# One transformer block, 16 chunks: the next chunk's first layer norm moves to the end of the current slot, and the query products open each slot

## The chip, the core and the metric

The kernel runs on one core of a Trainium2 chip. Its engines are TensorE (PE: matrix products and transposes into PSUM), VectorE (DVE), ScalarE (ACT), GpSimd (POOL) and SyncE (SP: the DMA queue). Each engine takes its own list of instructions in order; they meet at semaphores. The metric is the device time of one execution in microseconds (us).

## The reference

A cross-attention block on x (8, 1024, 512) with a context of 64 rows per batch, 16 heads of 32, and a feed-forward width of 2048:

```python
q = _layer_norm(query, ln1_g, ln1_b)
qh = (q @ wq + bq).reshape(Bq, Sq, H, hd)
kh = (context @ wk + bk).reshape(Bq, Sc, H, hd)
vh = (context @ wv + bv).reshape(Bq, Sc, H, hd)
scores = jnp.einsum('bqhd,bkhd->bhqk', qh, kh) * scale
scores = jnp.where(allowed[None, None, :, :], scores, NEG_INF)
probs = jax.nn.softmax(scores, axis=-1)
o = jnp.einsum('bhqk,bkhd->bqhd', probs, vh).reshape(Bq, Sq, Dm)
x = query + (o @ wo + bo)
h = _layer_norm(x, ln2_g, ln2_b)
return x + jax.nn.gelu(h @ w1 + b1, approximate=False) @ w2 + b2
```

## The kernel before

The 8192 rows of x are cut into 16 chunks of 512 rows, and a chunk into four tiles t of 128 rows. The program is a row of 17 slots. Slot c does the attention half of chunk c and, beside it, the feed-forward half of chunk c-1; slot 0 has attention only, slot 16 feed-forward only. Two slots (an even and an odd chunk) make one batch and one turn of a hardware loop. Products are in float16 with each operand split in a high and a low part, so that a product takes three matmuls per block of 128 rows.

A slot runs over 18 groups g. In group g TensorE does F1(g), the first feed-forward product (12 matmuls at line 989, g below 16), and F2(g-2), the second one (12 matmuls at line 1193, g from 2). Between them stand the attention steps. The table `PLAN` gives each step a position: position 2g comes after F1(g), position 2g+1 after F2(g-2). Every engine walks the same table, so it sets the order on all of them. The steps are, for each tile or head group t:

- T: the normalised rows `xhat` of chunk c are transposed (line 1032, four transposes), copied by ScalarE (line 578) and split by VectorE (line 711 into `act_T`). `xhat` has two buffers.
- Q: query products; S: scores, with VectorE's row maxima and subtraction (lines 920, 922); E: ScalarE's exponentials (line 590), VectorE's sums (line 927), and GpSimd's division (line 485, `normalise`).
- Z: transposes of the probabilities; V: products with the values; O: output product, residual and the statistics of the second norm; H: transposes of the second norm's rows, like T.

After the step at position 2g, VectorE splits the gelu of group g (lines 962 and 711); F2(g) waits for that. Called "the split of g" below.

The first norm of chunk c is done by VectorE at the very start of slot c, ahead of position 0: for each tile `norm_stats` (lines 687, 689, 692), then GpSimd's power in `rstd_of` (line 421), then `norm_apply` (line 707) into `xhat`. For tiles 0 and 1 `norm_apply` follows the statistics two tiles later; for tiles 2 and 3 it follows T(0) and T(1), since the buffers must be read first. GpSimd's adding of the output bias to x (line 480) stands behind these norms, and with each new batch also the building of its key and value blocks (lines 464, 473). At the end of a slot VectorE adds the feed-forward result to the residual (line 976, four instructions).

Slot 1 also does the last conversions of the weights, at positions given by `conversions_at`.

Of the kernel before, what the change touches and what calls it, by code (L numbers as in the profile page):

```python
# [22 lines left out]
BATCH = 8  # L23
# [6 lines left out]
TT = CHUNK // P  # L30
HALF = CHUNK // 2
NCHUNK = BATCH * SQ // CHUNK
# [18 lines left out]
LAG = 2  # L51
GROUPS = NJ + LAG
PLAN = {
# [8 lines left out]
}  # L62

PLAN_FIRST = {
# [7 lines left out]
}  # L72
W2_SUMS_AT = (0, 1, 20, 21)

# [11 lines left out]
def cross_attention_block(nc, x, context, wq, wk, wv, bq, bk, bv, wo, bo,  # L86
# [5 lines left out]
    with ExitStack() as ctx:  # L92
# [72 lines left out]
        x_sb = sb("x_sb", [P, TT, D], F32)  # L165
# [94 lines left out]
        x_loaded = [sem(f"x_loaded{t}") for t in range(TT)]  # L260
# [58 lines left out]
        def plan(c, position):  # L319

            return (PLAN_FIRST if isinstance(c, int) and c == 0 else PLAN).get(position, [])

        def halves(c, t):


            return ff2_ps[:, 0:2, :] if isinstance(c, int) and c == 0 and t % 2 else at_ps[:, :, :]

        def slots(eng, slot, loads=False):


            slot(0, 0, True, False, 0)
            slot(1, 1, True, True, None)
            with eng.Fori(0, BATCH - 1 - loads) as i:
                slot(2 * i + 2, 0, True, True, i + 1)
                slot(2 * i + 3, 1, True, True, None)
            if loads:
                slot(NCHUNK - 2, 0, True, True, BATCH - 1)
                slot(NCHUNK - 1, 1, True, True, None)
            slot(NCHUNK, 0, False, True, None)

        block = ctx.enter_context(nc.Block())
# [1 line left out]
        @block.sync  # L343
        def _(sp):
            sp.dma_start(ctx_raw, ctx_rows).then_inc(ctx_loaded, 16)
            sp.dma_start(wk_raw, wk.rearrange("(k p) n -> p k n", p=P)).then_inc(w_loaded[W_K], 16)
            row = 0
            for v in (bq, bk, ln1_g, ln1_b, ln2_g, ln2_b, b1):
                n = v.shape[0] // P
                sp.dma_start(vec_rows[row:row + n, :], v.rearrange("(k p) -> k p", p=P)).then_inc(vecs_loaded, 16)  # L350
                row += n
            sp.dma_start(wv_raw, wv.rearrange("(k p) n -> p k n", p=P)).then_inc(w_loaded[W_V], 16)
            sp.dma_start(bv_row, bv.rearrange("(a n) -> a n", a=1).to_broadcast([P, D])).then_inc(bv_loaded, 16)
            sp.dma_start(wq_raw, wq.rearrange("(k p) n -> p k n", p=P)).then_inc(w_loaded[W_Q], 16)
            for t in range(TT):
                sp.dma_start(x_sb[:, t], x_tiles[t]).then_inc(x_loaded[t], 16)
            for v, dst in ((bo, bo_row[:, :]), (b2, b2_row[:, :])):
                sp.dma_start(dst, v.rearrange("(a n) -> a n", a=1).to_broadcast([P, D])).then_inc(rows_loaded, 16)
            sp.dma_start(wo_raw, wo.rearrange("(k p) n -> p k n", p=P)).then_inc(w_loaded[W_O], 16)
            for n in range(N1):  # L360
                sp.dma_start(w1_raw[n], w1[:, n * D:(n + 1) * D].rearrange("(k p) n -> p k n", p=P)
                             ).then_inc(w_loaded[W_1 + n], 16)

            def load_w2(n):
                sp.dma_start(w2_raw[n], w2[n * D:(n + 1) * D, :].rearrange("(k p) n -> p k n", p=P)
                             ).then_inc(w_loaded[W_2 + n], 16)

            for n in W2_ORDER[:2]:
                load_w2(n)

            def move_values(n, batches):


                even, odd = slice(batches.start, batches.stop, 2), slice(batches.start + 1, batches.stop, 2)
                sp.wait_ge(kv_out, KT + batches.stop // 2)
                for a in range(2):
                    for half in (slice(0, SC), slice(SC, P)):
                        sp.dma_start(v_sb[half, a, odd, :], v_sb[SC:P, a, even, :]).then_inc(v_moved, 16)
                sp.wait_ge(v_moved, (6 * n + 4) * 16)
                for a in range(2):  # L380
                    sp.dma_start(v_sb[SC:P, a, even, :], v_sb[0:SC, a, even, :]).then_inc(v_moved, 16)

            move_values(0, slice(0, 2))
            move_values(1, slice(2, BATCH))
            for n in W2_ORDER[2:]:
                load_w2(n)

            def slot(c, par, attn, ff, batch):
                if not isinstance(c, int) or c < NCHUNK - 1:
                    for t in range(TT):  # L390
                        sp.wait_ge(x1_set, 4 * c + t + 1)
                        sp.dma_start(x_sb[:, t], x_tiles[4 * c + (TT + t)]).then_inc(x_loaded[t], 16)
                if ff:
                    for t in range(TT):
                        sp.wait_ge(out_set, 4 * c + (t + 1 - TT))
                        sp.dma_start(out_tiles[4 * c + (t - TT)], x1[1 - par][:, t]).then_inc(out_stored[t], 16)

            slots(sp, slot, loads=True)
            for t in range(TT):
                sp.wait_ge(out_stored[t], 16 * NCHUNK)  # L400

        @block.gpsimd
        def _(pool):
# [48 lines left out]
            def slot(c, par, attn, ff, batch):  # L452
                if not attn:
                    return
                first = isinstance(c, int) and c == 0
                if not first:
                    for t in range(TT):
                        rstd_of(c, t)

                def key_blocks():  # L460

# [56 lines left out]
                for t in range(TT):  # L518
                    rstd_of(c, TT + t)
                    if t:  # L520
                        add_b2(t - 1)
                add_b2(TT - 1)

            slots(pool, slot)

        @block.scalar
        def _(act):
# [104 lines left out]
            def slot(c, par, attn, ff, batch):  # L632
                first = isinstance(c, int) and c == 0
                for g in range(GROUPS):
                    if first and 2 * g == BIAS_ROWS_AT:
                        bias_rows(1, D, bias_rows_sb)
                    if first and 2 * g == CONV_FROM:
                        act.wait_ge(scales_ready[2], 1)
                    if ff and g < NJ:
                        act.wait_ge(ff1_done, NJ * c + (g + 1 - NJ))  # L640
                        if g >= 2:
                            act.wait_ge(g_lo, NJ * c + (g - 1 - NJ))
                        else:
                            wait(act, g_lo, NJ * c + (-NJ))
                        nc.scalar.activation(gelu_full[g % 2], ff1_ps[:, g % 2, :], ACT.Gelu,  # L645
                                             bias=b1p[:, g:g + 1], scale=col(C1)).then_inc(g_full, 1)
                    for position in (2 * g, 2 * g + 1):
                        if attn:
                            for kind, t in plan(c, position):
                                step(c, par, kind, t)  # L650
                        for n in conversions_at(c, position):
                            convert(n)
                        if first and position in W2_SUMS_AT:
                            n = W2_SUMS_AT.index(position)
                            magnitudes(W_2 + W2_ORDER[n], n + 1)
                if first:
                    act.wait_ge(scales_ready[3], 1)
# [4 lines left out]
        def _(dve):  # L662
# [228 lines left out]
                    convert(n)  # L891

            def slot(c, par, attn, ff, batch):
                if attn and not (isinstance(c, int) and c == 0):
                    for t in range(TT):
                        dve.wait_ge(x_loaded[t], 16 * (c + 1))
                        norm_stats(c, t, x_sb[:, t])
                        if t >= 2:
                            norm_apply(c, t - 2, x_sb[:, t - 2])

                def step(kind, t):
                    bank = at_ps[:, t % 2, :]
                    tiles = bank.rearrange("p (k n) -> p k n", k=KT)
                    if kind == "T":
                        T_step(c, t)
                    elif kind == "H":
                        dve.wait_ge(h_hi, 4 * c + t + 1)
                        rows = slice(t * P, (t + 1) * P)
# [73 lines left out]
        def _(pe):  # L982
# [93 lines left out]
            def slot(c, par, attn, ff, batch):  # L1076
                def step(kind, t):
                    bank = at_ps[:, t % 2, :]
                    rows = slice(t * P, (t + 1) * P)
                    if kind == "T":  # L1080
                        T_step(c, t)
                    elif kind == "W":
                        values(t)
                    elif kind == "Q":
# [137 lines left out]
```

## Time and profile before

| | us |
|---|---|
| median of three runs (2073.62 to 2075.64) | 2074.24 |
| the profiled execution's own time | 2073.56 |
| its span in the trace | 2071.8 |
| TensorE busy | 1942.1 (94%) |
| VectorE busy | 1291.9 (62%) |
| ScalarE busy | 589.0 (28%) |
| GpSimd busy | 452.9 (22%) |

The chain that ended last is 73% TensorE and 16% VectorE. Matmuls are pipelined: a group's busy times overlap, so distances between starts are what a block costs. In the timeline the number in brackets behind a row is how long the engine sat idle before it, and what released it.

### The profile page before, as it was taken

How to read it: one execution, taken by the hardware profiler on the slowest of the kernel's cores; microseconds unless marked ns; L12 is line 12 of the kernel's file. 1: busy time of each engine (PE TensorE's matmuls, PEld its weight loads, DVE VectorE, ACT ScalarE, POOL GpSimd, SP SyncE). 2: the span in 40 equal slices, each digit the busy share in tenths (PEclk: the TensorE clock that was granted, in tenths of full speed). 3: DMA queues.
4: the chain of work that ended last, by engine and by line, in shares of the span. 5: the costliest groups of instructions: out<-in, count | busy, mean ns of one | idle time of the engine just before them, and what ended most of it. 6: DMA issues, size and time to landing. Idle time of an engine off the chain costs nothing.

```text
span 2071.8 us, 28444 instructions
## 1 busy us (share of the span) xinstructions
PE 1942.1 (94%) x11206; PEld 965.0 (47%) x11206; DVE 1291.9 (62%) x1972; ACT 589.0 (28%) x820; POOL 452.9 (22%) x380
## 2 busy tenths in 40 slices
PE   4679999999999999999999999999999999999999
PEld 2334445445444444544445454544544454454444
DVE  5777766665656675666666566676666666556542
ACT  3544323232232312223232222313213231222311
POOL 2430231311222131211412022131122214111210
PEclk7879999999999999999999999999999999999999
DMA  7110000101000010000101000010100001000000
GB/s 259 37 56 1 16 26 1 41 1 31 12 11 31 1 42 1 21 21 6 36 1 41 1 21 22 1 41 1 42 1 16 26 1 42 1 23 19 1 21 21
DMA packets 27648, 51.32 MB, mean 25 GB/s; under 512 B 2536, under 2 KB 4112, under 8 KB 27536
## 3 DMA queue, kind: packets, MB, share of 16 engines
q1 hardware_dynamic: 27536, 49.58, 7.3%
q8 instruction: 101, 1.65, 0.3%
q14 instruction: 11, 0.09, 0.0%
HBM read 31.22 MB, written 16.78 MB: 23 GB/s over the span
## 4 chain that ended last, share of the span: by engine, by line
PE 73%; DVE 16%; issue 5%; ACT 3%; DVEq 2%; POOL 0%; DMA 0%; SPq 0%; POOLq 0%; ACTq 0%
PE ff_ps L1193 25%; PE ff_ps L989 24%; PE at_ps L989 15%; PE at_ps L1032 4%; DVE ssum L927 3%; DVE arena L962 3%; PE at_ps L1136 2%; PE at_ps L1110 2%; DVE arena L711 2%; DVEq L688 2%; DVE act_T L711 1%; DVE xhat L707 1%; ACT L590 1%; DVE arena L976 1%; ACT arena L590 1%
## 5 line engine op out<-in xcount | busy, mean ns | idle before, releaser
L1193 PE MATMUL ff_ps<-w_all,arena 128*128 128x512 f16 x3072 | 706.8, 380 | 31.4 <-DVE arena L711 27.1
L989 PE MATMUL ff_ps<-arena,w_all 128*128 128x512 f16 x3072 | 706.8, 381 | 3.9 <-issue 2.3
L1193 PEld LDWEIGHTS ff_ps<-w_all,arena 128*128 128x128 f16 x3072 | 295.5, 98 | 375.2 <-DVE arena L711 30.4
L989 PEld LDWEIGHTS ff_ps<-arena,w_all 128*128 128x128 f16 x3072 | 297.4, 98 | 349.8 <-issue 15.7
L645 ACT ACTIVATE arena<-ff_ps,b1p,scales 128x512 f32<-128x512 f32 x256 | 199.1, 778 | 852.4 <-PE ff_ps L989 762.6
L711 DVE SCALAR_TENSOR_TENSOR arena<-arena,scales 128x512 f16<-128x512 f32 x256 | 279.3, 1091 | 9.1
L485 POOL TENSOR_TENSOR arena<-arena,rsum 128x1024 f32<-128x1024 f32 x64 | 122.7, 1949 | 694.7 <-DVE rsum L930 694.7
L421 POOL TENSOR_TENSOR rstd<-ve,minus_half 128x1 f32<-128x1 f32 x128 | 90.6, 708 | 708.4 <-DVE ve L692 700.7
L962 DVE TENSOR_SCALAR arena<-arena,scales 128x512 f16<-128x512 f32 x256 | 159.8, 624 | 69.6 <-ACT arena L645 69.6
L711 DVE SCALAR_TENSOR_TENSOR arena<-at_ps,arena 128x512 f16<-128x512 f32 x188 | 123.8, 686 | 109.6 <-ACT arena L596 57.3
L989 PE MATMUL at_ps<-wo_hi,act_T 128*128 128x512 f16 x512 | 162.2, 379 | 1.5 <-DVE act_T L711 1.5
L989 PE MATMUL at_ps<-act_T,wq_hi 128*128 128x512 f16 x512 | 152.4, 379 | 7.2 <-DVE act_T L711 7.2
L914 DVE CAST qT<-arena 128x512 f16<-128x512 f32 x64 | 27.3, 427 | 199.2 <-ACT arena L583 199.2
L947 DVE SCALAR_TENSOR_TENSOR arena<-at_ps,scales,x_sb 128x512 f32<-128x512 f32 x64 | 48.0, 751 | 142.2 <-PE at_ps L989 142.2
L920 DVE TENSOR_REDUCE smax<-at_ps 128x16 f32<-128x1024 f32 x62 | 75.8, 1222 | 76.1 <-PE at_ps L1110 76.1
L1032 PE MATMUL at_ps<-ident,xhat 128*128 128x128 f32 x512 | 81.0, 282 | 44.6 <-DVE xhat L707 37.9
L711 DVE SCALAR_TENSOR_TENSOR act_T<-at_ps,act_T 128x512 f16<-128x512 f32 x128 | 85.3, 685 | 55.6 <-ACT act_T L602 55.6
L927 DVE TENSOR_REDUCE ssum<-arena 128x16 f32<-128x1024 f32 x64 | 75.3, 1177 | 54.1 <-ACT arena L590 54.1
L583 ACT ACTIVATE arena<-at_ps,bqp,scales 128x512 f32<-128x512 f32 x64 | 49.8, 778 | 198.2 <-PE at_ps L989 198.2
L480 POOL TENSOR_TENSOR x_sb<-x_sb,bo_row 128x512 f32<-128x512 f32 x64 | 95.7, 1513 | 19.8 <-DVE xhat L707 19.6
L1032 PEld LDWEIGHTS at_ps<-ident,xhat 128*128 128x128 f32 x512 | 63.4, 144 | 73.6 <-DVE act_T L711 26.0
L989 PE MATMUL at_ps<-act_T,wq_lo 128*128 128x512 f16 x256 | 97.0, 379 | 0.0
(136 smaller groups left out, 1595.0 us busy)
## 6 DMA issues: line engine op xcount, KB each, us to landing
x_sb<-in_x SPq DMA_DIRECT2D x64, 256.0 KB, 2.6
out_x<-arena SPq DMA_DIRECT2D x64, 256.0 KB, 2.2
w_all<-in_L_xattn_w SPq DMA_DIRECT2D x6, 1024.0 KB, 15.2
arena<-in_L_xattn_w SPq DMA_DIRECT2D x2, 1024.0 KB, 14.0
v_sb<-v_sb SPq DMA_DIRECT2D x6, 192.0 KB, 3.0
arena<-in_ctx SPq DMA_DIRECT2D x1, 1024.0 KB, 5.4
arena<-in_L_xattn_wk SPq DMA_DIRECT2D x1, 1024.0 KB, 8.1
arena<-in_L_xattn_wv SPq DMA_DIRECT2D x1, 1024.0 KB, 7.6
```

The lines of the kernel that those rows point to most:

```text
L421: nc.gpsimd.tensor_tensor(rstd[:, n:n + 1], ve[:, n:n + 1], minus_half[:, :], ALU.pow).then_inc(ln_rstd, 1)
L480: nc.gpsimd.tensor_tensor(x_sb[:, t], x_sb[:, t], bo_row[:, :], ALU.add).then_inc(xb_set, 1)
L485: nc.gpsimd.tensor_tensor(pr, pr, rsum[:, t, :].unsqueeze(2).to_broadcast([P, HEADS, SC]), ALU.mult).then_inc(p_norm, 1)
L583: nc.scalar.activation(q_full[t % 2], bank, ACT.Identity, bias=bqp[:, t:t + 1], scale=col(CQ)).then_inc(q_out, 1)
L645: nc.scalar.activation(gelu_full[g % 2], ff1_ps[:, g % 2, :], ACT.Gelu, bias=b1p[:, g:g + 1], scale=col(C1)).then_inc(g_full, 1)
L711: nc.vector.scalar_tensor_tensor(lo, src, factor, hi, ALU.mult, ALU.subtract).then_inc(done, 1)
L920: nc.vector.tensor_reduce(smax[:, t, :], scores, AX_X, ALU.max).then_inc(s_max, 1)
L927: nc.vector.reduce_sum(ssum[:, t, :], probs[t].rearrange("p (h k) -> p h k", k=SC), AX_X).then_inc(s_sum, 1)
L962: nc.vector.tensor_scalar(pair[:, 0, :], gelu_full[g % 2], col(SG), None, ALU.mult).then_inc(g_hi, 1)
L989: last = nc.tensor.matmul(out_ap, s, m, start=(i == 0), stop=(i == n - 1))
L1032: last = nc.tensor.transpose(bank[:, k * P:(k + 1) * P], source[:, k * P:(k + 1) * P], ident[:, :])
L1193: last = nc.tensor.matmul(ff2_ps[:, t, :], pair[:, s, rows], m[:, j], start=(j == 0 and i == 0), stop=(j == NJ - 1 and i == 2))
```

## The change

Slot c no longer begins with its own first norm. A new kind of step, M, does `norm_stats` of the next chunk's tile t and, from tile 2, `norm_apply` of tile t-2. M stands at positions 30 and 31, and the T steps of the next chunk at 32 to 35. With positions 0 to 5 free of T, the query products open the slot, and all the other steps come three positions earlier. Since positions move by an odd number, a step that stood behind F1 now stands behind F2 and the other way round. GpSimd's four powers for the next chunk come behind its last work of the second norm. Slot 0 gets M and T of chunk 1 at positions 27 and 28. The last chunk has no next one, so the last attention slots are now written out on every engine, and the loop has six turns.

```diff
 PLAN = {
-    2: [("T", 0)], 4: [("T", 1)], 5: [("T", 2), ("T", 3)],
-    6: [("Q", 0)], 7: [("Q", 1)], 8: [("Q", 2)], 9: [("Q", 3)],
...
+    0: [("Q", 0)], 2: [("Q", 1)], 4: [("Q", 2)], 5: [("Q", 3)],
...
+    27: [("H", 1)], 28: [("H", 2)], 30: [("H", 3), ("M", 0), ("M", 1)],
+    31: [("M", 2), ("M", 3)],
+    32: [("T", 0)], 33: [("T", 1)], 34: [("T", 2)], 35: [("T", 3)],
 }
...
+    27: [("M", 0), ("M", 1), ("M", 2), ("M", 3)],
+    28: [("T", 0), ("T", 1), ("T", 2), ("T", 3)],
...
+        def has_next(c):
+
+            return not isinstance(c, int) or c < NCHUNK - 1
...
-            with eng.Fori(0, BATCH - 1 - loads) as i:
+            with eng.Fori(0, BATCH - 2) as i:
...
-                if not first:
-                    for t in range(TT):
-                        rstd_of(c, t)
...
                 add_b2(TT - 1)
+                if has_next(c):
+                    for t in range(TT):
+                        rstd_of(c + 1, t)
...
-                if attn and not (isinstance(c, int) and c == 0):
-                    for t in range(TT):
-                        dve.wait_ge(x_loaded[t], 16 * (c + 1))
-                        norm_stats(c, t, x_sb[:, t])
-                        if t >= 2:
-                            norm_apply(c, t - 2, x_sb[:, t - 2])
-
...
+                    if kind == "M":
+                        if has_next(c):
+                            dve.wait_ge(x_loaded[t], 16 * (c + 2))
+                            norm_stats(c + 1, t, x_sb[:, t])
+                            if t >= 2:
+                                norm_apply(c + 1, t - 2, x_sb[:, t - 2])
+                    elif kind == "T":
+                        if has_next(c):
+                            T_step(c + 1, t)
```

**First place: VectorE, from the last steps H to the first norm.** Before, this is the turn from an even to an odd slot in the loop; line 711 from `at_ps` is the splitting of H(2) and H(3), line 976 the adding of the feed-forward result, and lines 687 to 692 the statistics of tile 0. REGISTER_ALU and ISA rows compute wait values and do no tile's work.

```order
L962 TENSOR_SCALAR arena<-arena,scales 128x512
L711 SCALAR_TENSOR_TENSOR arena<-arena,scales 128x512
L711 SCALAR_TENSOR_TENSOR arena<-at_ps,arena 128x4x128 x2
L972 REGISTER_ALU
L976 SCALAR_TENSOR_TENSOR arena<-ff_ps,scales,arena 128x512
L972 REGISTER_ALU
L976 SCALAR_TENSOR_TENSOR arena<-ff_ps,scales,arena 128x512 x3
L896 ISA
L687 BN_STATS stats<-x_sb 128x6
L689 BN_AGGR mv<-stats 128x2
```

Of the change, the same place in slot 1 (line 720 is the old 711, 696 to 701 the old 687 to 692, 716 the old 707, 971 the old 962). The first row is H(3)'s splitting.

```order
L720 SCALAR_TENSOR_TENSOR arena<-at_ps,arena 128x4x128
L696 BN_STATS stats<-x_sb 128x6
L698 BN_AGGR mv<-stats 128x2
L701 TENSOR_SCALAR ve<-mv 128x1
L696 BN_STATS stats<-x_sb 128x6
L698 BN_AGGR mv<-stats 128x2
L701 TENSOR_SCALAR ve<-mv 128x1
L971 TENSOR_SCALAR arena<-arena,scales 128x512
L720 SCALAR_TENSOR_TENSOR arena<-arena,scales 128x512
L696 BN_STATS stats<-x_sb 128x6
L698 BN_AGGR mv<-stats 128x2
L701 TENSOR_SCALAR ve<-mv 128x1
```

The statistics now stand between H(3) and the adding at the slot's end, two tiles ahead of the split of 15 and two behind it; `norm_apply` of tile 0 (line 716) is the next row.

**Second place: TensorE at the slot's end.** Before, in slot 1, line 1032 on `xhat` is H(0) to H(3) one after the other, and the slot ends with F2(15).

```order
L1032 MATMUL at_ps<-ident,xhat 128x128 x4
L989 MATMUL ff_ps<-arena,w_all 128x512 x12
L1032 MATMUL at_ps<-ident,xhat 128x128 x4
L1193 MATMUL ff_ps<-w_all,arena 128x512 x12
L1032 MATMUL at_ps<-ident,xhat 128x128 x4
L1193 MATMUL ff_ps<-w_all,arena 128x512 x12
L1032 MATMUL at_ps<-ident,xhat 128x128 x4
L1193 MATMUL ff_ps<-w_all,arena 128x512 x12
```

Of the change (998 is the old 989, 1203 the old 1193, 1041 the old 1032), from F2(12):

```order
L1203 MATMUL ff_ps<-w_all,arena 128x512 x12
L998 MATMUL ff_ps<-arena,w_all 128x512 x12
L1041 MATMUL at_ps<-ident,xhat 128x128 x4
L1203 MATMUL ff_ps<-w_all,arena 128x512 x12
L1041 MATMUL at_ps<-ident,xhat 128x128 x4
L1203 MATMUL ff_ps<-w_all,arena 128x512 x12
L1041 MATMUL at_ps<-ident,xhat 128x128 x8
L1203 MATMUL ff_ps<-w_all,arena 128x512 x12
L1041 MATMUL at_ps<-ident,xhat 128x128 x4
```

Behind F1(15) stand H(3), F2(13), T(0) of the next chunk, F2(14), T(1) and T(2), F2(15), T(3). Between H(3) and T(0) there is one block, F2(13).

**Third place: VectorE around the sums (E).** Before, in the loop, from the step S(3) (lines 920, 922), without what lies behind the second sum:

```order
L920 TENSOR_REDUCE smax<-at_ps 128x16
L922 TENSOR_TENSOR arena<-at_ps,smax 128x1024
L927 TENSOR_REDUCE ssum<-arena 128x16
L930 RECIPROCAL rsum<-ssum 128x16
L927 TENSOR_REDUCE ssum<-arena 128x16
```

Of the change, in the loop (929, 931, 936, 939 are the old 920, 922, 927, 930):

```order
L929 TENSOR_REDUCE smax<-at_ps 128x16
L931 TENSOR_TENSOR arena<-at_ps,smax 128x1024
L969 REGISTER_ALU
L971 TENSOR_SCALAR arena<-arena,scales 128x512
L720 SCALAR_TENSOR_TENSOR arena<-arena,scales 128x512
L936 TENSOR_REDUCE ssum<-arena 128x16
```

The split of 6 now stands between S(3) and the sums. The split behind the sums is that of 7; before it was that of 8.

## Rows read from the trace of the kernel before

**Rows 1.** The page: busy time of each engine.

```profile
PE 1942.1 (94%) x11206; PEld 965.0 (47%) x11206; DVE 1291.9 (62%) x1972; ACT 589.0 (28%) x820; POOL 452.9 (22%) x380
```

**Rows 2.** Who waited for whom, in total: us, times, longest.

```profile
PE at_ps L1032 <- DVE xhat L707: 37.9, 19, 11.1
...
PE ff_ps L1193 <- DVE arena L711: 27.1, 14, 1.9
...
PE at_ps L989 <- DVE act_T L711: 8.7, 8, 1.5
```

**Rows 3.** Timeline of TensorE, start of slot 8: start, us, what, idle before.

```profile
1016.82 0.60 PE L1032 MATMUL at_ps<-ident,xhat 128*128 128x128 f32 x4
1019.40 0.65 PE L1032 MATMUL at_ps<-ident,xhat 128*128 128x128 f32 x4 [1.98 <-DVE xhat L707]
1019.89 4.44 PE L989 MATMUL ff_ps<-arena,w_all 128*128 128x512 f16 x12
```

**Rows 4.** Windows: busy us of each engine, granted clock, DMA share, GB/s.

```profile
1020.05:1024.30 4.25, 4.25 (x14) 1.60 (x12) 3.45 (x4) 0.60 (x1) 3.41 (x3) 0.60 0.02 4
```

**Rows 5.** Timelines of TensorE and VectorE around the sums, slot 8.

```profile
1061.01 0.84 PE L1110 MATMUL at_ps<-arena,qT 64*128 64x128 f16 x24
1073.38 1.97 DVE L962 TENSOR_SCALAR arena<-arena,scales 128x512 f16<-128x512 f32 x1
1075.39 2.27 DVE L711 SCALAR_TENSOR_TENSOR arena<-arena,scales 128x512 f16<-128x512 f32 x1
1077.72 2.76 PE L1193 MATMUL ff_ps<-w_all,arena 128*128 128x512 f16 x12 [1.93 <-DVE arena L711]
```

**Rows 6.** Timeline of TensorE, slot 1: the wait for a weight's conversion.

```profile
217.32 4.44 PE L1193 MATMUL ff_ps<-w_all,arena 128*128 128x512 f16 x12 [4.14 <-DVE w_all L711]
```

**Rows 7.** Timelines of TensorE, ScalarE and VectorE at slot 8's end, around H(1).

```profile
1120.12 0.60 PE L1032 MATMUL at_ps<-ident,xhat 128*128 128x128 f32 x4
1123.14 0.60 PE L1032 MATMUL at_ps<-ident,xhat 128*128 128x128 f32 x4
...
1121.00 0.59 ACT L578 ACTIVATE arena<-at_ps 128x512 f16<-128x512 f32 x1
...
1121.62 0.69 DVE L711 SCALAR_TENSOR_TENSOR arena<-at_ps,arena 128x512 f16<-128x512 f32 x1 [1.35 <-ACT arena L578]
1122.22 0.54 DVE L707 TENSOR_SCALAR xhat<-arena,mv,rstd 128x512 f32<-128x512 f32 x1
```

**Rows 8.** Timelines of VectorE and GpSimd: statistics, powers, and one split.

```profile
1007.67 0.68 DVE L687 BATCH_NORM_STATS2 stats<-x_sb 128x6 f32<-128x512 f32 x1
1008.71 0.69 DVE L687 BATCH_NORM_STATS2 stats<-x_sb 128x6 f32<-128x512 f32 x1
1009.80 0.55 DVE L707 TENSOR_SCALAR xhat<-x_sb,mv,rstd 128x512 f32<-128x512 f32 x1
1018.39 0.88 DVE L707 TENSOR_SCALAR xhat<-x_sb,mv,rstd 128x512 f32<-128x512 f32 x1
1054.76 0.48 DVE L962 TENSOR_SCALAR arena<-arena,scales 128x512 f16<-128x512 f32 x1
1055.94 1.22 DVE L920 TENSOR_REDUCE smax<-at_ps 128x16 f32<-128x1024 f32 x1
...
1007.83 0.55 POOL L421 TENSOR_TENSOR rstd<-ve,minus_half 128x1 f32<-128x1 f32 x1 [7.60 <-DVE ve L692]
```

**Rows 9.** Timelines of TensorE and VectorE, from slot 0 to slot 1.

```profile
138.50 1.12 PE L1032 MATMUL at_ps<-ident,xhat 128*128 128x128 f32 x4 [0.51 <-DVE xhat L707]
141.12 7.88 PE L989 MATMUL ff_ps<-arena,w_all 128*128 128x512 f16 x24 [1.50 <-DVE arena L711]
157.26 0.66 PE L1032 MATMUL at_ps<-ident,xhat 128*128 128x128 f32 x4 [1.77 <-DVE xhat L707]
161.98 0.61 PE L989 MATMUL at_ps<-act_T,wq_hi 128*128 128x512 f16 x2 [1.47 <-DVE act_T L711]
...
145.24 0.55 DVE L707 TENSOR_SCALAR xhat<-x_sb,mv,rstd 128x512 f32<-128x512 f32 x1
```

More of the change, by code:

```diff
@@ L321, in plan, with slots @@
             return (PLAN_FIRST if isinstance(c, int) and c == 0 else PLAN).get(position, [])
+        def has_next(c):
+            return not isinstance(c, int) or c < NCHUNK - 1
         def halves(c, t):
             return ff2_ps[:, 0:2, :] if isinstance(c, int) and c == 0 and t % 2 else at_ps[:, :, :]
-        def slots(eng, slot, loads=False):
+        def slots(eng, slot):
             slot(0, 0, True, False, 0)
             slot(1, 1, True, True, None)
-            with eng.Fori(0, BATCH - 1 - loads) as i:
+            with eng.Fori(0, BATCH - 2) as i:
                 slot(2 * i + 2, 0, True, True, i + 1)
                 slot(2 * i + 3, 1, True, True, None)
-            if loads:
-                slot(NCHUNK - 2, 0, True, True, BATCH - 1)
-                slot(NCHUNK - 1, 1, True, True, None)
+            slot(NCHUNK - 2, 0, True, True, BATCH - 1)
+            slot(NCHUNK - 1, 1, True, True, None)
             slot(NCHUNK, 0, False, True, None)
@@ L396, in slot @@
                         sp.dma_start(out_tiles[4 * c + (t - TT)], x1[1 - par][:, t]).then_inc(out_stored[t], 16)
-            slots(sp, slot, loads=True)
+            slots(sp, slot)
             for t in range(TT):
@@ L649, in slot @@
                             for kind, t in plan(c, position):
-                                step(c, par, kind, t)
+                                if kind != "T":
+                                    step(c, par, kind, t)
+                                elif has_next(c):
+                                    step(c + 1, 1 - par, kind, t)
                         for n in conversions_at(c, position):
@@ L903, in step @@
                     tiles = bank.rearrange("p (k n) -> p k n", k=KT)
-                    if kind == "T":
-                        T_step(c, t)
+                    if kind == "M":
[7 more added lines that the diff above has]
+                            T_step(c + 1, t)
                     elif kind == "H":
@@ L1080, in step @@
                     if kind == "T":
-                        T_step(c, t)
+                        if has_next(c):
+                            T_step(c + 1, t)
                     elif kind == "W":
```

11 rows, old and new, of the table PLAN are left out of this document.

## The prediction

> **What bounds the kernel now.** The page first: TensorE is busy for 1942.1 of 2071.8 us [rows 1]. So time is lost only where TensorE stands idle or runs slowly, and the change adds or removes no matmul. What it can move is the waits. I read them in the table of who waited for whom, and then placed each in TensorE's timeline. Three kinds come back in every slot [rows 2]:
>
> - T(3) waits for VectorE's `norm_apply`. The total is 37.9 us in 19 waits. Four of them lie ahead of slot 1 (11.15, 0.70, 1.05 and 0.51, together 13.4), one is slot 1's 1.77 [rows 9]; the other 14, one for each of slots 2 to 15, sum to 22.7. They are 1.34 in odd slots and about 2 in even ones, where GpSimd builds key and value blocks beside VectorE; slot 8's is 1.98 [rows 3].
> - Q(0) waits for the last split of T. Of 8.7 us, 1.47 is slot 1's [rows 9] and one of 1.51 is the first O step's; 5.8 is left for the even slots.
> - F2(8) waits for the split of 8, which stands behind the four sums of E: 27.1 us, 14 times 1.93 [rows 2, 5].
>
> There is a fourth loss that no wait shows. In slot 8 the block behind T(3)'s wait took 4.44 us [rows 3], with a granted clock of 0.60 over those 4.25 us [rows 4]: most of it ran at the lower of the two levels, 1.2 GHz, and the rest at 2.4. The same 12 matmuls take 2.75 elsewhere, so it lost 1.69. Before it TensorE had stood for 1.98 us between transposes. Of the seven even slots only this one shows it. The other case is slot 1: after an idle stretch of 4.14 us its F2 block also took 4.44 [rows 6]. Waits of 1.93 and 1.34 never did it.
>
> Slots 2 to 15 thus lose 22.7 + 5.8 + 27.1 + 1.7 = 57.3 us that the new order could touch.
>
> **The change, part by part.**
>
> *The waits at T(3) and Q(0) at the slot's start go.* Q(0) needs the last split of T(3). In the new order F1(0), 2.6 us, lies between T(3) and Q(0). The path is T(3)'s transposes, ScalarE's copy and VectorE's split: from the start of the transposes to the end of the split's turn 2.1 us (the H steps have the same shape: 1120.12 to 1122.22) [rows 7], which is under 0.44 + 2.6. The additions of line 976 come behind that split. So Q(0) costs nothing.
>
> *The wait at F2(8) goes.* The cover is counted in blocks. A block of 12 matmuls costs 2.59 (1123.14 less 1120.12 is 3.02, of which 0.43 is the transposes) [rows 7]. Before, S(3) starts at 1061.01 and the split of 8 ends at 1077.66, 16.65 later, while five blocks, S(3) and Z(0) bring TensorE to F2(8) after 14.8 [rows 5]. In the new order the split held up by the sums is that of 7. It is needed by F2(7), which stands behind one block and one Z step more: 14.8 + 2.59 + 0.87 = 18.2. The chain on VectorE is the same plus one split ahead of the sums, 1.18 (1054.76 to 1055.94) [rows 8]; at worst 16.65 + 1.18 = 17.8. It should be earlier, since before the sums VectorE was idle for ScalarE's exponentials, which now start one gelu sooner. Both ends are under 18.2. If the cover failed, the wait would be tenths, up to the 1.93 of today.
>
> *A new wait comes at T(0).* This is the term that decides. TensorE works on H(3), then F2(13), then wants T(0). Everything T(0) needs stands behind H(3) on VectorE, by the order printed above: H(3)'s split, statistics of tiles 0 and 1, the split of 15, statistics of tile 2, then `norm_apply` of tile 0. From H(3)'s start as zero:
> - H(3)'s split starts at 1.50 and the next instruction at 2.10. This is H(1) of today, which also follows F1(15), with a gelu ahead of its copy [rows 7].
> - statistics of tile 0 and 1: 1.05 each (1007.67 to 1008.71) [rows 8], to 4.20.
> - the split of 15: 1.18, to 5.38.
> - statistics of tile 2 up to the start of `norm_apply`: 1.09 (1008.71 to 1009.80) [rows 8], to 6.47; GpSimd's power for tile 0 takes 0.55 [rows 8] and began before 4, so it is not awaited.
> - `norm_apply` 0.55, to 7.02; from its end to the transposes 0.13 (1018.39 + 0.88 to 1019.40) [rows 3, 8], to 7.15.
>
> TensorE is free at 3.02. The new wait is 4.13 us. Behind it in TensorE's list stand F2(14), whose operands are ready, T(1), T(2) and F2(15), so all of it is late, and the next slot with it. T(1) to T(3) then find their rows ready: T(1) has F2(14)'s 2.59 in front, T(3) has F2(15). The x rows are loaded after each residual of step O, far ahead, so no DMA is awaited. GpSimd's bias additions to x now run beside the T splits; they take the last 0.3 us off no slack I can find on the path.
>
> Is VectorE idle where this could have been done? Yes, but in order: between the split of 14 and H(3) it waits for H(3)'s transposes, and the statistics stand behind that.
>
> *Sum of slots 2 to 15.* New waits: slots 2 to 14 have a next chunk, 13 x 4.13 = 53.7, against 57.3. Slot 15 has no T any more, 4 x 0.43 = 1.7 less. Together -3.6 - 1.7 = -5.3.
>
> *Slots 0 and 1.* Chunk 1's norm now stands at the end of slot 0, where TensorE has nothing beside it. VectorE's `norm_apply` for tile 0 is at 145.24 today and its list up to there is unchanged. So T(0) starts at 145.9. At the low clock the transposes take 1.12 [rows 9]. T(2) comes after T(0), copy (0.60), split (0.69), apply (0.55) and their gaps, near 149.2. T(1) is ready 1.6 after T(0), and T(3) follows it by the same chain, near 150.6, ending at 151.8. Today slot 1 begins at 141.12 [rows 9], so +10.7. Slot 1 then saves its T (1.7), its waits 1.77 and 1.47 [rows 9], and the 4.14 with its 1.69 [rows 6]: F2(8) there waits for a conversion at position 18, and now stands behind Z(2) instead of Z(0), several blocks later against the same conversion. It gains T of chunk 2 (1.7) and a new wait at T(0), 4.13. Net 10.7 - 1.7 - 3.2 - 5.8 + 1.7 + 4.1 = +5.8.
>
> *Without any effect on the clock* the whole is -5.3 + 5.8 = +0.5 us: a tie.
>
> *The clock.* Fourteen waits of 4.13 us replace fourteen of 1.3 to 2.2. The nearest row in length is slot 1's 4.14, which was followed by a slow block [rows 6]; the row nearest in kind, a wait beside T, did it once in seven at about 2 us [rows 3]. A slow stretch costs 1.69 each time. Bounds: none of 14, +0; all 14, +23.7. The longer wait speaks for many, but the one row at 4.14 is one row. I take the middle between 1 in 7 and 1 in 1, 8 of 14: +13.5.
>
> The Trainium skill, TensorE: Matmul & The Clock Gate, section HAM oscillation, says that an idle gap in each round of a loop puts the engine back to the half rate each time, so that the cost is paid every round. By that all 14 would lose, which is the rival below; the trace agrees for the gap of 4.14 us, and for one of the seven near 2.
>
> Forecast: 2073.6 + 0.5 + 13.5 = 2087.6 for an execution like the profiled one. That one lies 0.7 under the median of the runs, so 2088.3.
>
> **The rivals.**
>
> 1. *Every gap loses the clock*: 2074.24 + 0.5 + 23.7 = 2098.4. For it: rows 6 and the page. Against: six of seven gaps near 2 us cost nothing, so it depends on more than that there is a gap. 20%.
> 2. *No clock effect* (at most two of the 14 gaps): 2074.7, up to 2078. The moves cancel. For it: the gap is broken by T(0)'s transposes, and gaps of 1.93 never lost anything. Against: rows 6. 14%.
> 3. *Faster*: the new wait is no longer than today's 1.98. The place is VectorE's list at the slot's end: if H(3) came early enough, or the statistics were not in one chain with the split of 15, T(0) would wait 1.98 and the clock would hold: 2074.7 - 14 x (4.13 - 1.98) = 2044.6. It decides below 4.1 us, if the clock holds. Against it stands the printed order, in which none of the five pieces can pass another. 8%.
> 4. *The cover of the sums fails, or GpSimd is late*: F2(7) waits 1.93 too, 14 times, 27 more: 2115. Against: 18.2 is above both ends, and GpSimd has only the powers to do there. 6%.
>
> The forecast, 3 to 12 of the 14 gaps followed by a slow block, has the remaining 52%, and gives 2080 to 2095.
>
> **How the numbers follow.** A measurement of this kernel tells 0.2%, 4.1 us, from no change. Faster: rival 3, 8%. Within 0.2%: rival 2 and a small part of the forecast, 16%. Slower: the rest, 76%. The range: from 2072.5, rival 2 with a few us of error in the start, to 2100, rival 1. That leaves out rivals 3 and 4.
>
> **What would show each step.** In the new profile TensorE's wait for line 716 should total some 58 us in 14 waits beside those of the start, each near 4.1, at the first T behind H(3). The waits of line 1203 for a split (27.1) and of the query product (5.8) should be gone. The slow block should be F2(14), 4.4 instead of 2.75, in about half the slots. Slot 1 should start near 152. The prediction is wrong if the wait at T(0) is under 3.5 or over 5, if a wait is left at F2(7), or if the clock stays full in all slots.

## The result and the profile after

| | before | after |
|---|---|---|
| median, lowest to highest, us | 2073.93, 2073.3 to 2075.64 | 2105.51, 2103.87 to 2110.23 |
| runs | 4 | 4 |
| profiled execution, us (span) | 2073.62 (2071.8) | 2110.23 (2108.4) |

The ratio is 1.0153, with a 95% interval of 1.0141 to 1.0165: 31.6 us slower. The direction was forecast. The size was not, and 2105.51 lies above the range. The profiled execution of the changed kernel is the slowest of its four, 4.7 us over the median, so the trace has 36.6 us to account for where the medians differ by 31.6.

The page and the table of waits come first. The old lines 989, 1032 and 1193 are now 998, 1041 and 1203; 707 and 711 are 716 and 720. These rows answer to [rows 1, 2]:

```profile
PE 1962.5 (93%) x11206; PEld 975.2 (46%) x11206; DVE 1246.8 (59%) x1972; ACT 589.3 (28%) x820; POOL 435.3 (21%) x380
L998 PE MATMUL ff_ps<-arena,w_all 128*128 128x512 f16 x3072 | 709.7, 381 | 15.9 <-issue 15.9
```

```profile
PE at_ps L1041 <- DVE xhat L716: 77.3, 22, 12.2
PE ff_ps L998 <- issue: 15.9, 5, 3.4
```

The waits at F2(8) (27.1) and at Q(0) have left the table. The wait at the norm doubled from 37.9. TensorE's busy time rose by 20.4 us with the same 11206 matmuls, so some of them ran more slowly. And there is a row that the prediction does not have: 15.9 us of idle "issue" in front of the feed-forward's first product (F1), in five pieces. Below, a turn of the loop is the jump from the end of its body back to the start: six of them before, five now, since the last two attention slots are written out.

TensorE's timeline shows all of it at the end of slot 7, where the loop turns:

```profile
1015.93 0.60 PE L1041 MATMUL at_ps<-ident,xhat 128*128 128x128 f32 x4
1016.37 2.75 PE L1203 MATMUL ff_ps<-w_all,arena 128*128 128x512 f16 x12
1023.07 0.65 PE L1041 MATMUL at_ps<-ident,xhat 128*128 128x128 f32 x4 [3.95 <-DVE xhat L716]
1023.56 4.44 PE L1203 MATMUL ff_ps<-w_all,arena 128*128 128x512 f16 x12
1027.83 1.04 PE L1041 MATMUL at_ps<-ident,xhat 128*128 128x128 f32 x8
1028.71 2.75 PE L1203 MATMUL ff_ps<-w_all,arena 128*128 128x512 f16 x12
1031.30 0.60 PE L1041 MATMUL at_ps<-ident,xhat 128*128 128x128 f32 x4
1035.13 5.30 PE L998 MATMUL ff_ps<-arena,w_all 128*128 128x512 f16 x12 [3.23 <-issue]
```

H(3), F2(13), then T(0) after 3.95 us of idle time; F2(14) slow at 4.44; T(1) and T(2), F2(15), T(3); then 3.23 us for which the profile shows no wait, and F1(0) at 5.30 in place of 2.75. VectorE's timeline over the same place gives the chain that T(0) waits for:

```profile
1017.43 0.69 DVE L720 SCALAR_TENSOR_TENSOR arena<-at_ps,arena 128x512 f16<-128x512 f32 x1 [3.74 <-ACT arena L584]
1018.04 0.68 DVE L696 BATCH_NORM_STATS2 stats<-x_sb 128x6 f32<-128x512 f32 x1
1019.08 0.68 DVE L696 BATCH_NORM_STATS2 stats<-x_sb 128x6 f32<-128x512 f32 x1
1020.12 0.48 DVE L971 TENSOR_SCALAR arena<-arena,scales 128x512 f16<-128x512 f32 x1
1020.64 0.75 DVE L720 SCALAR_TENSOR_TENSOR arena<-arena,scales 128x512 f16<-128x512 f32 x1
1021.30 0.69 DVE L696 BATCH_NORM_STATS2 stats<-x_sb 128x6 f32<-128x512 f32 x1
1022.39 0.55 DVE L716 TENSOR_SCALAR xhat<-x_sb,mv,rstd 128x512 f32<-128x512 f32 x1
...
1029.71 1.07 DVE L716 TENSOR_SCALAR xhat<-x_sb,mv,rstd 128x512 f32<-128x512 f32 x1
```

It is the order of the prediction, piece by piece: H(3)'s split, two tiles of statistics, the split of 15, the third tile, `norm_apply`. From H(3)'s start to T(0)'s it takes 7.14 us (1015.93 to 1023.07); 7.15 was worked out. The first of these rows also shows 3.74 us in which VectorE had nothing to do, right ahead of the chain.

The windows of two stretches (columns as in [rows 4]) show the clock:

```profile
1023.07:1028.00 4.93, 4.93 (x18) 2.25 (x19) 2.97 (x6) 0.60 (x1) 4.21 (x5) 0.65 0.00 2
1035.13:1040.40 5.27, 5.27 (x13) 1.88 (x14) 0.76 (x2) 0.00 (x0) 0.00 (x0) 0.50 0.54 193
```

Behind T(0) the granted clock is 0.65, a mixture of the two levels. Behind the turn it is 0.50 for the whole 5.27 us: 1.2 GHz and nothing else.

What TensorE does in the 3.23 us stands in the view of the loop's own line, 340 (before: 333). It lists what TensorE's sequencer does there, the part that reads its list of instructions and runs ahead of the matmuls. The first row is the changed kernel's, the second the old one's; the three times are the shortest, the median and the longest in ns:

```profile
L340 PEldq COMPARE_BRANCH  x6: 83/3752/3835, 529.9 to 1782.9; - x6
L333 PEldq COMPARE_BRANCH  x7: 83/3512/3863, 512.0 to 1981.9; - x7
```

The 83 ns are the last pass, which leaves the loop. Each of the others is a jump back, and it holds the sequencer for 3.3 to 3.9 us, in the old kernel as in the new one. In the new one, at the end of slot 7, T(3)'s rows are ready at 1030.78, the branch starts at 1031.0, and TensorE has matmuls only until 1031.90. In the old one the branch at the same turn starts at 1001.8, and TensorE has matmuls until 1005.30: 3.5 us of work lie over it, and 0.28 us are left to see.

**Where the time went.** The span grew by 36.6 us. I place it by the starts of TensorE's instructions. From chunk 2's T(0) to chunk 15's T(0) the kernel before took 1593.4 us (275.82 to 1869.22) and this one takes 1623.7 (274.50 to 1898.16): +30.3. In this stretch:

- waits: 13 new ones, each 7.14 less 3.02, some 4.11 us by starts, are 53.5; the old ones, measured the same way, were 57.5. -4.0.
- clock at T(0): F2(14) was slow at all 14 waits. From T(0) to T(3) a slot without loss takes 6.54; these took 7.88 to 9.07, 21.8 too much for the 13. Before it was 1.7. +20.1.
- turns of the loop: 15.9 idle, and two slow F1(0) of 4.11 and 5.30 in place of 2.75 (3.9), against 2.3 idle before, in five short gaps (one of the six turns shows none). +17.5.

That makes 33.6, 3.3 more than the distance; the rest lies in small pieces that I have not placed. Outside the stretch the two T(0) have to be aligned first: the new one comes ahead of four blocks (F2(14), F2(15), F1(0), F1(1), 10.5 us) that the old one came after. The start is then 274.50 + 10.5 - 275.82 = 9.2 us longer. Of that 3.7 arose before H(0) of slot 0 (at 136.10, before at 132.43), ahead of anything that the change moves; 5.5 belongs to slots 0 and 1. The end is 210.2 - 202.6 - 10.5 = 2.9 us shorter.

### The profile page after: what moved, and what is told of

Its sections match the earlier page's. It is cut to its first block, busy times and chain, and to the rows that moved or that the text cites. A ratio compares the mean times of both kernels' runs of the same rounds, so it can differ in the third digit from the quotient of the medians.

```text
span 2108.4 us, 28365 instructions
## 1 busy us (share of the span) xinstructions
PE 1962.5 (93%) x11206; PEld 975.2 (46%) x11206; DVE 1246.8 (59%) x1972; ACT 589.3 (28%) x820; POOL 435.3 (21%) x380
## 4 chain that ended last, share of the span: by engine, by line
PE 87%; DVE 5%; issue 3%; DVEq 2%; ACT 2%; POOL 1%; DMA 0%; SPq 0%; POOLq 0%; ACTq 0%
PE ff_ps L998 32%; PE ff_ps L1203 30%; PE at_ps L998 15%; PE at_ps L1041 5%; PE at_ps L1146 2%; PE at_ps L1120 2%; DVEq L697 2%; DVE arena L720 1%; DVE xhat L716 1%; DVE mv L698 0%; DVE ssum L936 0%; ACT arena L584 0%; DMA arena<-in_L_xattn_wv 0%; ACT arena L651 0%; DVE maxima L729 0%
## 5 line engine op out<-in xcount | busy, mean ns | idle before, releaser
L1203 PE MATMUL ff_ps<-w_all,arena 128*128 128x512 f16 x3072 | 725.9, 388 | 0.0
L998 PE MATMUL ff_ps<-arena,w_all 128*128 128x512 f16 x3072 | 709.7, 381 | 15.9 <-issue 15.9
L1203 PEld LDWEIGHTS ff_ps<-w_all,arena 128*128 128x128 f16 x3072 | 302.3, 100 | 351.6 <-issue 31.0
L720 DVE SCALAR_TENSOR_TENSOR arena<-arena,scales 128x512 f16<-128x512 f32 x256 | 240.8, 941 | 9.1
L971 DVE TENSOR_SCALAR arena<-arena,scales 128x512 f16<-128x512 f32 x256 | 144.6, 565 | 90.5 <-ACT arena L651 90.5
L998 PE MATMUL at_ps<-wo_lo,act_T 128*128 128x512 f16 x256 | 97.1, 379 | 0.0
L493 POOL TENSOR_TENSOR arena<-arena,b_row 128x512 f32<-128x512 f32 x64 | 84.2, 1316 | 33.7 <-DVE xhat L716 33.7
```

Source lines behind the costliest of these rows:

```text
L493: nc.gpsimd.tensor_tensor(x1[par][:, t], x1[par][:, t], b2_row[:, :], ALU.add).then_inc(x1b_set, 1)
L720: nc.vector.scalar_tensor_tensor(lo, src, factor, hi, ALU.mult, ALU.subtract).then_inc(done, 1)
L971: nc.vector.tensor_scalar(pair[:, 0, :], gelu_full[g % 2], col(SG), None, ALU.mult).then_inc(g_hi, 1)
L998: last = nc.tensor.matmul(out_ap, s, m, start=(i == 0), stop=(i == n - 1))
L1203: last = nc.tensor.matmul(ff2_ps[:, t, :], pair[:, s, rows], m[:, j], start=(j == 0 and i == 0), stop=(j == NJ - 1 and i == 2))
```

## The experiments

Two costs were to be tested. The clock: each wait of 4.1 us makes the block behind it slow, about 22 us. The turn: the loop's jump is no longer hidden, since T(3), the last thing before it, has a wait; about 18 us. "Theory A" and "Rival B" in the expectations are each run's own. The first four kernels ran on one chip, where the kernel before took 2076.97 (2075.75 to 2080.36), the last three on another, where it took 2078.02 (2074.8 to 2079.6). Every ratio is to these.

**e1_fill.** The wait stays, but TensorE works in it: 18 products of 512 columns whose result nothing reads.

```diff
+FILLER = 18
...
             def T_step(c, t):
+                if t == 0 and not (isinstance(c, int) and c < 2):
+                    pe.wait_ge(h_lo, 4 * c + (t - 1))
+                    for n in range(FILLER):
+                        nc.tensor.matmul(at_ps[:, 0, :], wq_hi[:, 0, 0:P], wo_hi[:, 0], start=True, stop=True)
                 pe.wait_ge(ln_out, 8 * c + t + 1)
```

The added `wait_ge` is one that T(0) has anyway.

> The changed kernel, and in front of T(0) of chunks 2 to 15 TensorE does 18 matmuls of 512 columns (3.9 us at the full clock) whose result nobody reads, while it would otherwise wait for VectorE's row. Nothing else is changed. Theory A (the wait itself is set by VectorE and costs 4.1 us, and the idle stretch costs the clock on top, some 1.6 us each): T(0) starts when it did, F2(14) takes 2.75 again instead of about 4.4, and the time falls by 14 x 1.6 = 22 us, from 2105.5 to about 2083. Rival B (the slow block has another cause, for instance the transposes or the VectorE and GpSimd traffic beside it): the block stays slow and the time stays at 2105.

Measured: 2089.3 (2083.33 to 2093.92), ratio 1.005 (1.0032 to 1.0068). That is 12.3 over its kernel before, where the changed one is 31.6 over its own: 19 us back. The slow blocks behind T(0) are gone in all slots, as here in TensorE's timeline at the end of slot 7:

```profile
1009.89 4.05 PE L1050 MATMUL at_ps<-wo_hi,wq_hi 128*128 128x512 f16 x18
1013.93 0.66 PE L1042 MATMUL at_ps<-ident,xhat 128*128 128x128 f32 x4
1014.42 2.75 PE L1208 MATMUL ff_ps<-w_all,arena 128*128 128x512 f16 x12
...
1023.42 2.84 PE L999 MATMUL ff_ps<-arena,w_all 128*128 128x512 f16 x7 [2.34 <-issue]
1027.13 2.29 PE L999 MATMUL ff_ps<-arena,w_all 128*128 128x512 f16 x5 [0.87 <-issue]
```

T(0) starts no earlier (7.06 behind H(3)), so what came back is the clock alone. Forecast were 22 us; the four runs lie 10.6 us apart, and the interval alone is 3.7 us to either side, so the medians do not tell 19 from 22. The trace does: from T(0) to T(3) all 14 slots now take 6.54 to 6.60 where they lost 23.2 us in all, while the turns got dearer. A second gap opens inside F1(0), and F1(0) is slow, in part at least, at all five; by starts the five turns cost 27.0 us in place of 19.8, of which 17.8 are idle, in ten pieces. Why the gap splits is open.

**e2_unroll.** The changed kernel with the loop written out.

```diff
-            with eng.Fori(0, BATCH - 2) as i:
+            for i in range(BATCH - 2):
```

> The changed kernel with all slots written out and no hardware loop. Theory A (TensorE's gap of 3.2 us behind T(3), five times, and the slow blocks behind it come from the loop's jump, which TensorE's sequencer can only begin once T(3)'s wait has cleared): the five gaps vanish with their clock loss, 15.9 + 4.3 = 20 us, about 2085. Rival B (the gap is a wait for h, for the stores or for code in general): the gaps stay or come back at every slot, 2105 or more. The waits at T(0), 4.1 each, stay.

Measured: 2083.82 (2082.49 to 2087.28), ratio 1.0032 (1.0018 to 1.0046): 6.9 over its kernel before, so writing the loop out was worth some 25 us (20 forecast); the trace places 20 of them at the turns. No "issue" gap is left, while the T(0) waits and the slow F2(14) are what they were. At the end of slot 7 TensorE's timeline now reads:

```profile
1014.57 1.12 PE L1041 MATMUL at_ps<-ident,xhat 128*128 128x128 f32 x4 [3.85 <-DVE xhat L716]
1015.48 3.91 PE L1203 MATMUL ff_ps<-w_all,arena 128*128 128x512 f16 x12
...
1022.69 0.60 PE L1041 MATMUL at_ps<-ident,xhat 128*128 128x128 f32 x4
1023.13 2.75 PE L998 MATMUL ff_ps<-arena,w_all 128*128 128x512 f16 x12
```

F1(0) follows T(3) by 0.44 us, not by 3.83.

**e3_norm_early.** The chain on VectorE is moved, not shortened: three tiles of statistics go to position 29, where VectorE had been idle, ahead of H(3).

```diff
-    27: [("H", 1)], 28: [("H", 2)], 30: [("H", 3), ("M", 0), ("M", 1)],
-    31: [("M", 2), ("M", 3)],
+    27: [("H", 1)], 28: [("H", 2)], 29: [("M", 0), ("M", 1), ("M", 2)],
+    30: [("H", 3)], 31: [("M", 3)],
```

> The changed kernel with M(0), M(1), M(2) at position 29, ahead of H(3), and M(3) at 31. VectorE is idle there for 3.7 us and the three take about 3.7. Theory A (T(0)'s wait is only the place of the statistics behind H(3)): the wait is gone in all 14 slots and the clock loss with it: 14 x 4.1 + 22 = 79 us less, 2026; the loop's gaps stay. Rival B (GpSimd's powers, the x rows or H(3)'s later split are next in line): a wait of 1 to 2 us stays at T(0), T(1) or the next slot's Q(0), 2040 to 2060.

Measured: 2026.73 (2025.29 to 2027.2), ratio 0.9757 (0.9741 to 0.9773), as forecast if the wait at T(0) is only the place of the statistics: 50 us faster than before, by moving two entries of a table. In slots 2 to 15 T waits 0.22 to 0.30, in every other slot, and the only slow blocks there are at two turns. One of them, from TensorE's and then VectorE's timeline:

```profile
748.13 0.60 PE L1041 MATMUL at_ps<-ident,xhat 128*128 128x128 f32 x4
751.31 4.22 PE L998 MATMUL ff_ps<-arena,w_all 128*128 128x512 f16 x12 [2.58 <-issue]
...
746.26 0.95 DVE L716 TENSOR_SCALAR xhat<-x_sb,mv,rstd 128x512 f32<-128x512 f32 x1
```

T(3)'s `norm_apply` ends at 747.21, and 4.10 us later F1(0) starts.

**e4_t_late.** T is put off instead: T(0) and T(1) to position 33, T(2) and T(3) to 35, so that more blocks lie ahead.

```diff
-    32: [("T", 0)], 33: [("T", 1)], 34: [("T", 2)], 35: [("T", 3)],
+    33: [("T", 0), ("T", 1)], 35: [("T", 2), ("T", 3)],
```

> The changed kernel with T(0), T(1) at position 33 and T(2), T(3) at 35, so that F2(14) fills 2.6 us of the wait. Theory A: T(0) waits about 1.5 and T(1) about 1.2, the clock is kept as in the gaps of that size before, so 14 x 1.4 + 22 = 42 us less, 2063. Rival B (any wait at this place loses the clock): only 14 x 1.4 = 20 less, 2086.

Measured: 2061.7 (2059.84 to 2064.32), ratio 0.9929 (0.9912 to 0.9946). One wait of 3.95 became two, about 1.4 and 0.8. TensorE's timelines at the ends of slots 2 and 7:

```profile
392.30 0.65 PE L1041 MATMUL at_ps<-ident,xhat 128*128 128x128 f32 x4 [1.37 <-DVE xhat L716]
393.74 0.66 PE L1041 MATMUL at_ps<-ident,xhat 128*128 128x128 f32 x4 [0.79 <-DVE xhat L716]
394.23 4.44 PE L1203 MATMUL ff_ps<-w_all,arena 128*128 128x512 f16 x12
...
999.72 0.65 PE L1041 MATMUL at_ps<-ident,xhat 128*128 128x128 f32 x4 [1.36 <-DVE xhat L716]
1001.17 0.66 PE L1041 MATMUL at_ps<-ident,xhat 128*128 128x128 f32 x4 [0.80 <-DVE xhat L716]
1001.67 2.75 PE L1203 MATMUL ff_ps<-w_all,arena 128*128 128x512 f16 x12
```

The same two waits lost the clock in 3 slots of 14 and kept it in 11. So it is not the presence of a wait at T that costs the clock.

**e5_early_unroll.** The edits of e3_norm_early and e2_unroll together.

> The statistics moved ahead of H(3) (M(0), M(1), M(2) at 29, M(3) at 31) and all slots written out: both cures together. Theory A (two separate costs, the wait at T(0) with its clock and the loop's jump): the effects add up. From 2026.7 the five gaps of 2.4 to 2.9 behind T(3), with 0.17 each that the trace hides, and two slow blocks of 1.5 go: 13.1 + 0.9 + 3 = 17 us, about 2010, and no wait above 0.4 is left in slots 2 to 15. Rival B (one hides behind the other): less than half of it, 2018 or more.

Measured: 2009.8 (2008.4 to 2012.42), ratio 0.9671 (0.9655 to 0.9687). It is the fastest version, 68 us under the kernel before and 18 further under it than e3_norm_early (17 forecast): the two cures add up. In slots 2 to 15 one wait at T of 0.57 us is left, the others are 0.23 or less. The end of slot 6 in TensorE's timeline:

```profile
860.48 0.60 PE L1041 MATMUL at_ps<-ident,xhat 128*128 128x128 f32 x4
861.31 0.66 PE L1041 MATMUL at_ps<-ident,xhat 128*128 128x128 f32 x4 [0.22 <-DVE xhat L716]
861.80 2.75 PE L1203 MATMUL ff_ps<-w_all,arena 128*128 128x512 f16 x12
864.39 0.60 PE L1041 MATMUL at_ps<-ident,xhat 128*128 128x128 f32 x4
864.83 2.75 PE L998 MATMUL ff_ps<-arena,w_all 128*128 128x512 f16 x12
```

**e6_before_unroll.** Is the written-out loop simply better? The kernel before, with all slots written out in the same way.

> The kernel before with all slots written out, nothing else. Theory A (the jump costs some 4.2 us from the last wait that TensorE's sequencer has to pass, and before the change 3.7 us of queued matmuls cover it): only the rest of 0.2 to 0.65 at each of six turns goes, 2 to 3 us, 2071 to 2075 against 2074 to 2077 for the kernel before on the same chip. Rival B (the loop itself costs 3 us a turn in every kernel, hidden from the trace): 15 to 20 us less.

Measured: 2079.99 (2076.98 to 2082.59), ratio 1.0014 (1.0004 to 1.0023). It gains nothing, where the rival expected 15 to 20 us, so the turn's cost is hidden in the old order and shows in the new one. The 2 to 3 us forecast did not come either; it came out 2 us slower. Its waits at T(3) in even slots are 2.2 throughout, and the slow block of [rows 3] stands in five of seven even slots instead of one, such as this one in TensorE's timeline. Four more at some 1.7 each are more than the 2.3 us of idle time at the turns that went:

```profile
1022.24 1.12 PE L1029 MATMUL at_ps<-ident,xhat 128*128 128x128 f32 x4 [2.21 <-DVE xhat L704]
1023.15 3.97 PE L986 MATMUL ff_ps<-arena,w_all 128*128 128x512 f16 x12
```

**e7_before_turn_wait.** The opposite test: the kernel before, loop kept, with one wait at the end of odd slots, for a value that H(3)'s split sets anyway.

```diff
+                if attn and not isinstance(c, int) and par == 1:
+                    pe.wait_ge(h_lo, 4 * c + 4)
```

> The kernel before, and at the end of each odd slot in the loop TensorE's sequencer waits for H(3)'s split before it may jump. The next slot's first matmul waits for that split anyway, and it is done 1.1 us into F2(15), so nothing is delayed but the jump. Theory A (the jump costs about 4.2 us from the last wait passed): the gap at the six turns grows from 0.2 to 0.65 to about 3 us, 6 x 2.7 = 16 us, plus a slow block behind some of them, 0 to 8: 2090 to 2100. Rival B (the gap in the changed kernel comes from what its loop body contains or how long it is): no change, 2074 to 2077.

Measured: 2088.98 (2085.69 to 2091.74), ratio 1.0047 (1.003 to 1.0063): 11 us slower from one added wait, 1 us under the forecast. TensorE's timeline at the third turn, and the split that is awaited, from VectorE's:

```profile
1013.75 2.75 PE L1193 MATMUL ff_ps<-w_all,arena 128*128 128x512 f16 x12
1019.46 1.90 PE L989 MATMUL ff_ps<-arena,w_all 128*128 128x512 f16 x8 [2.96 <-issue]
...
1014.58 0.69 DVE L711 SCALAR_TENSOR_TENSOR arena<-at_ps,arena 128x512 f16<-128x512 f32 x1 [2.00 <-ACT arena L578]
```

The split ends at 1015.27, the branch starts at 1015.4 and takes 3.75, and F1(0) starts 4.19 behind the split. In the kernel before, by the same timelines (both rows of F1(0) end with the window that was asked for, hence 8 and 16 matmuls):

```profile
1002.12 0.60 PE L1032 MATMUL at_ps<-ident,xhat 128*128 128x128 f32 x4
1002.55 2.75 PE L1193 MATMUL ff_ps<-w_all,arena 128*128 128x512 f16 x12
1005.58 3.62 PE L989 MATMUL ff_ps<-arena,w_all 128*128 128x512 f16 x16 [0.28 <-issue]
...
999.14 1.64 DVE L711 SCALAR_TENSOR_TENSOR arena<-arena,scales 128x512 f16<-128x512 f32 x1
```

There the last wait in TensorE's list is F2(15)'s, for the split of 15, the last row; it ends at 1000.78, and the sequencer has F2(15) to hand on before it comes to the branch at 1001.8. The end of F2(14), H(3) and F2(15) fill all but 0.28 us. (The 4.2 us in two expectations were counted from the split of H(2), which ends at 1001.38 and which TensorE doesn't wait for there; the branch's own row is the better measure.) The six turns of e7_before_turn_wait idle for 16.9 us, and F1(0) with F1(1) took 7.04 or 6.86 instead of 5.35 behind four of them. Part of this was given back at once, since T(3) behind a turn then waited only 0.58 to 1.17. F2(8)'s wait of 1.94 us lost the clock in four slots here (4.45 for 2.76), which it never did before, so some 6.8 us of this kernel's time need not be the turn's own.

## Why the prediction was wrong

- *The wait at T(0).* Right: 4.13 us forecast, 4.11 measured by starts. Printed as idle time it is 3.95, as the old ones were printed too short as well.
- *The waits at T(3), Q(0), F2(8) go, and F2(7) stays covered.* Right; none has a row left in slots 2 to 15. Rival 4 fell with that, and rival 3, since all 14 waits came.
- *The slow block is F2(14).* Right in place, wrong in number. "I take the middle between 1 in 7 and 1 in 1, 8 of 14" was the mis-sized term: it was 14 of 14 here, and 14 of 14 in e2_unroll. The term was +13.5; the 14 measured 23.2 (the 20.1 above are 13 of them, less the old slow block). Taking the middle between two rows of different length was the error: the row of the same length, 4.14 us [rows 6], pointed to every slot. Rival 1 had this right.
- *The sum of slots 2 to 15* lacked a term, and this is the step that failed. The prediction walked through TensorE's matmuls and took the next slot to follow T(3) as the old one followed F2(15). "Behind it in TensorE's list stand F2(14), whose operands are ready, T(1), T(2) and F2(15)" stops one entry short: what stands behind T(3) in five slots is the loop's jump. Its sequencer reaches the jump only when T(3)'s wait has cleared, with the end of F2(15) and one group of transposes left to cover it. The rows to ask were in the old trace: the 0.28 <-issue ahead of slot 8's F1(0) (shown under e7_before_turn_wait), an idle piece that nothing awaited explains and so the end of a cost that is almost hidden, and the branch of line 333, 3.3 to 3.9 us at each turn. The prediction read neither and put the turn at nothing. +17.5 in the trace; e2_unroll returns it, e7_before_turn_wait makes it in the old kernel, e6_before_unroll shows that next to none of it was to be had there.
- *Slots 0 and 1.* The norm of chunk 1 cost 10.5 (10.7 forecast). Slot 1 started at 155.26, "near 152" once the loading phase's 3.7 is taken off. "F2(8) there waits for a conversion" and is freed: no. The conversions' backlog moved to the next step that waits, Z(1): 2.26 us and a slow block of 4.40. TensorE's timeline of slot 1, beside [rows 6]:

```profile
217.20 1.25 PE L1041 MATMUL at_ps<-ident,arena 128*128 128x128 f32 x8 [2.26 <-DVE arena L720]
218.24 4.40 PE L1203 MATMUL ff_ps<-w_all,arena 128*128 128x512 f16 x12
```

That is 3.9 us not forecast. They are nearly made up by a quicker start of slot 1 (3.48 for one block, where two took 7.88) and by small pieces, so the place as a whole came out at 5.5 where 4.1 was forecast up to the same point (5.8 less chunk 2's own transposes).

With the clock at 23.2 and the turns at 17.5 in place of 13.5 and nothing, the sum for the profiled execution would have been 2087.6 + 9.7 + 17.5 = 2114.8, against 2110.23, of which 3.7 is the later start that no term could have. So the two terms account for the miss, and overstate it by 8.3 us. 5.2 of that is a fault of the sum itself: it set the new waits, taken by starts, against the old ones as printed, each 0.17 too short; those of the 13 slots are 52.3 printed and 57.5 by starts. Most of the rest is the 3.3 that the ledger does not place. Without the 17.5 of the turns the median would be 2088.0, inside the range and next to the 2088.3 forecast, but by luck: the clock term was 9.7 too low and the rest as much too high.

What is shown: the clock term (e1_fill, with no change to the wait), the turn term (e2, e6, e7 and the branch's rows) and the cause of the wait (e3). What is only argued: that VectorE's late split in slot 1 is the conversions' backlog. What stays open: why waits of 1.4 to 2.2 us lose the clock in some slots and not in others, why the turn's gap splits in e1_fill, and what TensorE's sequencer spends the 3.3 to 3.9 us of a jump on.

## What to carry to other kernels

When a step with a wait is moved to the end of a hardware loop's body, count the jump: put the wait ahead of enough queued matmuls to cover it (3.3 to 3.9 us here), or write the loop out. When work is moved in front of a consumer, ask which idle stretch of the producing engine it could fill first; here the same statistics, placed one position earlier, turned a loss of 1.5% into a gain of 2.4%, and 3.3% with the loop written out. Price an idle gap on TensorE as the gap and the slow block behind it, by a row of the same length.

## What the runs showed of the hardware

- A jump back in TensorE's loop held its sequencer for 3.31 to 3.89 us at each of the 32 turns of six kernels; leaving the loop took 0.08. The next slot's first matmul started 3.57 to 4.15 us after the branch did. This is hidden only as far as TensorE still has matmuls to do when the branch starts: 3.5 us of them in the kernel before, where up to 0.65 us of idle time was left, and 0.65 to 1.28 in the four with a loop whose last wait comes late and stands unfilled (after, e3, e4, e7), where 2.4 to 3.4 was.
- After such a gap the first block was slow at two of five turns (after), two of five (e3), one of five (e4) and four of six (e7).
- Waits of 3.85 to 3.95 us were followed by a slow block, or slow transposes, in all 28 cases of two kernels (after, e2), at a loss of 1.3 to 2.5 us. Two waits of about 1.4 and 0.8 in a row did it in 3 of 14 (e4), a wait near 2 at T(3) of even slots in 1 of 7 (before) and 5 of 7 (e6), one of 1.94 at F2(8) in none of 14 (before) and 4 of 14 (e7). Work whose result is thrown away holds the clock as well as useful work.
- Idle time ahead of a TensorE instruction is counted from the modelled end of the one before. For the waits here that is 0.17 us less than the distance of the starts gives.
